# Keys and values of a four-layer attention kernel's third layer: computed in the layer itself, or ahead of it in the second

## The reference

```
q = layer_norm(x) @ q_w + q_b                # 16 heads of 32 columns
k = ctx @ k_w + k_b
v = ctx @ v_w + v_b
h = softmax(q k^T / sqrt(32)) v @ cproj_w + cproj_b + x
x = h + gelu(layer_norm(h) @ fc_w + fc_b) @ proj_w + proj_b
```

## Time and profile before

| | |
|---|---|
| median of three runs | 2687.87 us (2686.5 to 2689.95) |
| the profiled execution | 2687.89 us, span 2686.1 us |
| busy | PE 2477.0 (92%), DVE 1280.0, POOL 1106.1, ACT 1089.2 us |
| grouped layer | about 797 to 1198 us of the span |
| third layer's attention | about 1198 to 1537 us |
| mean granted TensorE clock | 0.967 of full speed |
| DMA | 181.25 MB, mean 67 GB/s |

### The profile page before, as it was taken

The page is one execution under the profiler, slowest core; times in us unless marked ns, Lnnn a source line. Parts: engine busy times, 40 slices in busy tenths (PEclk is TensorE's granted clock), DMA queues, the critical chain, the costliest instruction groups (busy, mean ns, idle before and its releaser), DMA issues.

```text
span 2686.1 us, 47930 instructions
## 1 busy us (share of the span) xinstructions
PE 2477.0 (92%) x18464; PEld 2080.4 (77%) x18464; DVE 1280.0 (48%) x2527; ACT 1089.2 (41%) x3705; POOL 1106.1 (41%) x1972
## 2 busy tenths in 40 slices
PE   7999998999997788758889899999899999899999
PEld 5887886888886666647778788888788888688887
DVE  4555564323226878764555533322355555432322
ACT  4555553111117777754565511111355555311111
POOL 2454446400035888873454571003335444640000
PEclk9999999999998989878999999999999999999999
DMA  4112213111122222221232241102211211311100
GB/s 154 56 56 74 86 48 95 59 47 48 57 71 72 82 91 70 74 67 45 94 111 77 82 129 48 47 23 69 87 48 49 84 53 48 95 59 48 47 32 16
DMA packets 110320, 181.25 MB, mean 67 GB/s; under 512 B 7888, under 2 KB 43408, under 8 KB 109072
## 3 DMA queue, kind: packets, MB, share of 16 engines
q1 hardware_dynamic: 110096, 178.19, 20.2%
HBM read 132.02 MB, written 46.14 MB: 66 GB/s over the span
## 4 chain that ended last, share of the span: by engine, by line
PE 79%; DVE 8%; ACT 6%; POOL 3%; issue 3%; DMA 1%; SPq 0%; DVEq 0%; POOLq 0%; ACTq 0%
PE banks L317 70%; PE banks L453 4%; ACT plain_high L697 4%; PE banks L480 3%; DVE neg_max L948 2%; DVE plain_high L944 2%; POOL plain_high L1268 1%; DVE plain_work L953 1%; PE banks L504 1%; DVE rounded_work L1046 1%; DVE rounded_work L1020 1%; DVE stats L1072 1%; POOL rounded_high L308 0%; PE banks L442 0%; ACT plain_high L684 0%
## 5 line engine op out<-in xcount | busy, mean ns | idle before, releaser
L317 PE MATMUL banks<-rounded_work,rounded_low 128*128 128x512 f32 (+1 forms) x2688 | 534.7, 357 | 58.4 <-issue 35.2
L1268 POOL TENSOR_SCALAR plain_high<-plain_high,inv_sum 128x128 f32<-128x128 f32 (+1 forms) x1024 | 389.6, 403 | 410.2 <-DVE inv_sum L966 409.7
L317 PEld LDWEIGHTS banks<-rounded_work,rounded_low 128*128 128x128 f32 x2688 | 446.7, 200 | 125.6 <-issue 53.7
L317 PE MATMUL banks<-rounded_work,rounded_high 128*128 128x512 f32 (+1 forms) x2400 | 485.4, 356 | 8.4 <-DMA rounded_work<-ctx_split 5.8
L925 ACT ACTIVATE plain_work<-banks,columns 128x512 f32<-128x512 f32 x192 | 132.5, 690 | 865.3 <-PE banks L317 865.3
L317 PEld LDWEIGHTS banks<-rounded_work,rounded_high 128*128 128x128 f32 x2400 | 397.1, 191 | 75.8 <-issue 10.0
L1244 DVE CAST rounded_work<-plain_work 128x512 fp32r<-128x512 f32 x192 | 99.3, 517 | 694.1 <-ACT plain_work L925 682.9
L317 PE MATMUL banks<-rounded_low,rounded_work 128*128 128x512 f32 x1728 | 413.1, 391 | 0.0
L317 PE MATMUL banks<-rounded_high,rounded_work 128*128 128x512 f32 (+1 forms) x1728 | 392.7, 380 | 0.0
L317 PEld LDWEIGHTS banks<-rounded_low,rounded_work 128*128 128x128 f32 x1728 | 322.3, 188 | 68.8 <-issue 3.0
L317 PEld LDWEIGHTS banks<-rounded_high,rounded_work 128*128 128x128 f32 x1728 | 311.8, 190 | 60.4 <-issue 1.4
(11 more groups left out here) (101 smaller groups left out, 3055.3 us busy)
## 6 DMA issues: line engine op xcount, KB each, us to landing
plain_work<-x SPq DMA_DIRECT2D x96, 256.0 KB, 2.8
plain_work<-mlp_w SPq DMA_DIRECT2D x96, 256.0 KB, 2.7
rounded_work<-ctx_split SPq DMA_DIRECT2D x24, 1024.0 KB, 5.9
u<-plain_work SPq DMA_DIRECT2D x48, 256.0 KB, 3.1
plain_work<-u SPq DMA_DIRECT2D x12, 1024.0 KB, 7.2
x<-plain_work SPq DMA_DIRECT2D x48, 256.0 KB, 2.1
plain_work<-attention_w SPq DMA_DIRECT2D x44, 256.0 KB, 2.7
plain_work<-inputs_t SPq DMA_DIRECT2D x8, 1024.0 KB, 8.0
```

The lines of the kernel that those rows point to most:

```text
L317: mm = pe.matmul(dst, lhs(i), rhs(j), start=first and n == 0, stop=last and n == 2, skip_group_check=True)
L1268: last = pool.tensor_scalar(part, part, inv_sum[:, R % 2, r, g:g + 1], 1.0, ALU.mult, ALU.mult)
```

## The change

The third layer's keys and values are computed in the grouped layer, where that layer's context is in `XC` anyway, a pair ahead. For each pair that is two key blocks (24 matmuls of 256 columns each), two value blocks (12 of 512 each), and their evacuation. For pair 0 all four stand at the grouped layer's start; for pair p+1 the key blocks stand behind attend of rounds 0 and 1 of pair p, the values behind attend of round 2 and behind the queries of round 3. The results go to `k_ahead` and `v_ahead`, in two slots that hold the third layer's output weights before, are stored to DRAM (1 MB and 0.5 MB a pair), and are loaded by the third layer into double buffers. In the third layer keys, values and the context load are gone, and the output of row 2p-1 stands ahead of attend of round 0 on TensorE, and on VectorE ahead of the heads. The grouped layer's next context load waits for the last value block. Weight splits move: the third layer's key and value weights to the end of the first MLP, four of its query tiles remain in the grouped layer, four output tiles go to the third layer's start.

The diff, cut (ScalarE's removals in the third layer, which mirror TensorE's, semaphores and index helpers are left out):

```diff
         KT_G = [work(rounded, 16 + 4 * h, 2, 2, 2 * P) for h in range(2)]
-        KT_C = work(rounded, 16, 2, 4, 2 * P)
+        KT_C = [work(rounded, 16 - 8 * h, 2, 4, 2 * P) for h in range(2)]
+        XT_C = work(rounded, 0, 2, FB, 2 * P)
+        k_ahead, v_ahead = slots(rounded, 6, 2, 4, 2 * P), slots(plain, 7, 2, D)
         QT = work(rounded, 48, 2, 4, 2 * P)
...
         y_of = [x_of[1], None, x_of[3], out]
+        keys_of, values_of = (nc.dram_tensor(n, [PAIRS, P, w], F32).ap() for n, w in (("cross_keys", 2048), ("cross_values", 1024)))
         ctx_split = nc.dram_tensor("ctx_split", [PAIRS, P, 2, FB, 2 * P], F32).ap()
...
 
-        for key in (("a", 0), ("m", 0), ("a", 1), ("a", 2), ("m", 2), ("a", 3), ("m", 3)):
-            tile_table[key] = (attention_tiles if key[0] == "a" else mlp_tiles)(L[key[1]])
+        for key, names in ((("a", 0), ("o",)), (("m", 0), None), (("a", 1), ("kv", "q")), (("kv", 2), ("k", "v")), (("o", 1), ("o",)),
+                           (("qo", 2), ("q", "o")), (("m", 2), None), (("a", 3), ("k", "v", "q", "o")), (("m", 3), None)):
+            tile_table[key] = mlp_tiles(L[key[1]]) if names is None else attention_tiles(L[key[1]], names)
             first_tile[key] = count
...
         def pe_queries(pe, y, p, i):
...
                 pe_weights(pe, y, "q")
+            if y.kind == CROSS and i == 0:
+                pe_inputs(pe, y, p)
+            x_t = XT_C if y.kind == CROSS else XC[:, :, :, 2 * P:4 * P]
             key = ("Q", y.n, p, i)
...
                     mm = three_passes(pe, dst[:, j * 256:j * 256 + 256], lambda h: weight(y, "q", h, f, t * P, t * P + P),
-                                      lambda h: XC[:, h, f, 2 * P:4 * P], f == 0, f == FB - 1)
+                                      lambda h: x_t[:, h, f, :], f == 0, f == FB - 1)
             mm.then_inc(filled_by(key), 1)
...
             else:
+                pe.wait_ge(kt_loaded[p % 2], 16 * (p // 2 + 1))
                 for i in range(2):
-                    wait_evac(pe, ("K", y.n, p, i))
                     wait_evac(pe, ("Q", y.n, p, i))
...
             pe_values(pe, y, 0, 0)
+            for i in range(2):
+                pe_keys(pe, L[2], 0, i)
+            for i in range(2):
+                pe_values(pe, L[2], 0, i)
             for p in range(PAIRS):
...
                     pe_keys(pe, y, p + 1, 0)
+                    pe_keys(pe, L[2], p + 1, 0)
                 pe_scores(pe, y, p, 2)
...
                 pe_attend(pe, y, p, 1)
+                if more:
+                    pe_keys(pe, L[2], p + 1, 1)
                 pe_scores(pe, y, p, 3)
...
                 if more:
+                    pe_values(pe, L[2], p + 1, 0)
                     pe_scores(pe, y, p + 1, 0)
...
                     pe_queries(pe, y, p + 1, 1)
+                    pe_values(pe, L[2], p + 1, 1)
             pe_out(pe, y, B - 1)
...
         def pe_cross(pe, y):
...
             for i in range(2):
-                pe_keys(pe, y, 0, i)
-            for i in range(2):
                 pe_queries(pe, y, 0, i)
             pe_scores(pe, y, 0, 0)
-            for i in range(2):
-                pe_values(pe, y, 0, i)
             for p in range(PAIRS):
...
                     pe_turn_x(pe, y, p + 1)
+                if p:
+                    pe_out(pe, y, 2 * p - 1)
                 pe_attend(pe, y, p, 0)
                 if more:
-                    for i in range(2):
-                        pe_keys(pe, y, p + 1, i)
                     for i in range(2):
...
                         pe_turn_u(pe, M[y.n], 0, f)
-                if p:
-                    pe_out(pe, y, 2 * p - 1)
                 if more:
...
                 pe_attend(pe, y, p, 1)
-                if more:
-                    for i in range(2):
-                        pe_values(pe, y, p + 1, i)
             pe_out(pe, y, B - 1)
...
             else:
+                if p and i == 0:
+                    act.wait_ge(k_stored, 16 * p)
                 for j in range(2):
                     t = 2 * i + j
-                    last = act.activation(KT_C[:, 0, t, :], bank(key)[:, j * 256:j * 256 + 256], ACT.Identity, bias=col(y, 4 + t))
+                    last = act.activation(k_ahead[:, 0, t, :], bank(key)[:, j * 256:j * 256 + 256], ACT.Identity, bias=col(y, 4 + t))
                 last.then_inc(hi_done, hi_count(key))
...
                     act_keys(act, y, p + 1, 0)
+                    act_keys(act, L[2], p + 1, 0)
                 act_round(act, y, p, 2, (p, 1), nothing)
...
                 act_heads(act, y, p, 1)
+                if more:
+                    act_keys(act, L[2], p + 1, 1)
                 act_round(act, y, p, 3, (p, 2), nothing)
...
                 act_heads(act, y, p, 2)
+                if more:
+                    act_values(act, L[2], p + 1, 0)
                 act_round(act, y, p + 1, 0 if more else None, (p, 3), nothing)
...
             dve_queries(dve, y, 0, 1)
+            for i in range(2):
+                dve_keys(dve, L[2], 0, i)
             dve.wait_ge(m_stored, 64 * GROUPS)
...
 
+                dve_values(dve, L[2], p, 1)
                 dve_round(dve, y, p, 1, (p, 0), inputs)
...
                     dve_keys(dve, y, p + 1, 0)
+                    dve_keys(dve, L[2], p + 1, 0)
                 dve_round(dve, y, p, 2, (p, 1), nothing)
...
                 dve_heads(dve, y, p, 1)
+                if more:
+                    dve_keys(dve, L[2], p + 1, 1)
                 dve_round(dve, y, p, 3, (p, 2), nothing)
...
                 more = p + 1 < PAIRS
-                dve_values(dve, y, p, 1)
 
                 def inputs():
...
                 dve_round(dve, y, p, 1, (p, 0), inputs)
+                if p:
+                    dve_out(dve, y, 2 * p - 1)
                 dve_heads(dve, y, p, 0)
                 if more:
-                    for i in range(2):
-                        dve_keys(dve, y, p + 1, i)
                     dve_mask(dve, y, p + 1)
...
                         dve_turn_u(dve, M[y.n], 0, f)
-                if p:
-                    dve_out(dve, y, 2 * p - 1)
                 dve_round(dve, y, p + 1, 0 if more else None, (p, 1), nothing)
...
                 pool_bias(pool, y, 2 * p)
-                split_tile(pool, ("a", 2), 2 * p)
+                if p < 4:
+                    split_tile(pool, ("qo", 2), p)
                 pool_norm(pool, y, p, 3)
-                split_tile(pool, ("a", 2), 2 * p + 1)
                 pool_bias(pool, y, 2 * p + 1)
...
         def pool_cross(pool, y):
+            pool.wait_ge(k_stored, 16 * PAIRS)
+            pool.wait_ge(v_stored, 16 * PAIRS)
+            split_tile(pool, ("qo", 2), 4)
+            split_tile(pool, ("qo", 2), 5)
             pool_norm(pool, y, 0, 0)
+            split_tile(pool, ("qo", 2), 6)
+            split_tile(pool, ("qo", 2), 7)
             for p in range(PAIRS):
...
                     split_tile(pool, ("a", 1), i)
+                pool.wait_ge(down_done, base + 8)
+                for i in range(8):
+                    split_tile(pool, ("kv", 2), i)
                 pool.wait_ge(down_done, base + 11)
-                for i in range(8, 12):
-                    split_tile(pool, ("a", 1), i)
+                for i in range(4):
+                    split_tile(pool, ("o", 1), i)
             elif y.n == 2:
...
 
+        def sp_keys_ahead(sp, p):
+            for i in range(2):
+                wait_evac(sp, ("K", 2, p, i))
+            sp.dma_start(keys_of[p], k_ahead.rearrange("p a b c -> p (a b c)").bitcast(F32)).then_inc(k_stored, 16)
+        def sp_values_ahead(sp, p):
+            for i in range(2):
+                wait_evac(sp, ("V", 2, p, i))
+            sp.dma_start(values_of[p], v_ahead.rearrange("p a b -> p (a b)")).then_inc(v_stored, 16)
+        def sp_ahead(sp, p):
+            sp_keys_ahead(sp, p)
+            sp_values_ahead(sp, p)
+        def sp_cross_keys(sp, p):
+            sp.dma_start(KT_C[p % 2].rearrange("p a b c -> p (a b c)").bitcast(F32), keys_of[p]).then_inc(kt_loaded[p % 2], 16)
+        def sp_cross_values(sp, p):
+            sp.dma_start(V_C[p % 2].rearrange("p a b -> p (a b)"), values_of[p]).then_inc(vc_loaded[p % 2], 16)
         def sp_gqa(sp, y):
...
                 sp.dma_start(t, ins[f"L1_xattn_{name}"].rearrange("(a n) -> a n", a=1).broadcast_to([P, D])).then_inc(gb_loaded, 16)
+            sp_ahead(sp, 0)
             for p in range(PAIRS):
...
                 if more:
-                    wait_filled(sp, v_last(y, p))
+                    wait_filled(sp, ("V", 2, p, 1))
                     sp_c(sp, y, p + 1)
...
                     sp_qk_mask(sp, p + 1)
-                load_tile(sp, ("a", 2), 2 * p)
-                load_tile(sp, ("a", 2), 2 * p + 1)
+                if p < 4:
+                    load_tile(sp, ("qo", 2), p)
                 if p:
+                    sp_values_ahead(sp, p)
                     sp_store_h(sp, y, 2 * p - 2)
...
```

(63 more changed lines are left out.)

36 lines of the change are left out of this document (18 added, 18 removed).

## The result

The changed kernel takes 2695.34 us (median of 8 executions, 2692.91 to 2699.35), the kernel before 2687.49 in the same session. The ratio is 1.0029 with an interval of 1.002 to 1.0039: slower by 0.3%, where 2671.0 and faster was forecast. The profiled execution took 2694.84 us, with a span of 2692.8 against 2686.1.

What follows compares the result with a forecast made beforehand. Four engines handing to one another bound the grouped layer, TensorE with almost no cover the third. Grouped layer and start +61.5 us, third layer -78, sum -16.5: 2671 us from 2687.87, range 2644 to 2704.

Steps and rivals of the forecast that it cites:

- the third layer, -78: Third layer: taking out keys and values saves 78 us, bounds -85 to -67.
- the first pair (-7.0): Third layer's first pair: only the keys go, queries start to end falling from 13.8 to 6.8 us, -7.0.
- the six pairs (-62.6): Third layer's six further pairs: each 29.5 us against 39.94, -10.4 a pair, -62.6 in all.
- the last M0 to M1 (-2.7): Third layer's last pair, between its two rows' first maxima on VectorE: -2.7 us without values.
- the piece with two bounds: Third layer's queries: 5.8 us at full clock, 8.0 with a slow first half, 6.8 taken.
- The rival of another wait in this layer: Third layer: in-order chains of ScalarE and VectorE hold the pair near 33 us, 2692 in all; chance 0.12.
- the full-clock sum of the grouped layer: Grouped layer's four rounds with added blocks at full clock: 53.0 us against 46.7, 53.9 on the average pair.
- the charge for the half clock: Grouped layer: half of a block's extra 2.2 us charged, making a pair 55.0 us, +7.4 a pair, +52.
- sign of being wrong: Grouped layer: a pair over 57.5 us would show the forecast wrong.
- the case of slow blocks: Rival, grouped layer: added blocks run slow, 2714 us in all by the author's estimate; chance 0.20.
- Nothing, as said: Grouped and third layers: added stores and loads, 1.5 MB a pair each, costed at nothing.
- The rival that the grouped layer hides more: Grouped layer: idle TensorE time takes added work, a pair of 52 us, 2645 in all; chance 0.13.

Runs made afterwards that it cites:

- e3: Changed kernel with the third layer's moved output projection and its copy put back at their old place in all pairs; 2704.66 us, ratio 1.0061.
- e2: Changed kernel with six useless 512-column matmuls ahead of attend of rounds 1 to 3 in grouped-layer pairs 0 to 6; 2665.91 us, ratio 0.9915.
- e1: Changed kernel with three of the four added grouped-layer blocks issued ahead of attend of rounds 1, 2 and 3, not behind; 2650.33 us, ratio 0.9859.
- e7: e1 with eight useless 512-column matmuls ahead of the first scores of each next pair in the third layer; 2647.65 us, ratio 0.9854.
- e4: Changed kernel with the output projection and its copy back at their old place in the third layer's last pair alone; 2695.41 us, ratio 1.0026.
- e5: e1 with the edit of e4 as well; ratio 0.9866, of three executions of 2649.79 to 2653.61 us.
- e6: Kernel before with the filler of e2, on the grouped layer's query weights; 2690.04 us, ratio 1.0021.

## Why the prediction was wrong

**Right: the third layer, -78.** Its terms came out at -5.8 for the start (forecast -5.9), -4.3 for the first pair (-7.0), -66.0 for the six pairs (-62.6) and -2.1 for the last M0 to M1 (-2.7): -78.2. That the sum agrees to 0.1 is luck: the first pair gave 2.7 less and the six pairs 3.4 more. The queries were the piece with two bounds and came out near the lower one, at 6.0 us, with a wait of 1.28 us ahead of them; in e3 they took 7.43 behind a wait of 3.24, so that both the shorter wait and the shorter queries came with the moved projection. The rival of another wait in this layer fell.

**Right: the full-clock sum of the grouped layer.** 53.9 us a pair was worked out from rows of the kernel before, and e2, which has the change's code at full clock, takes 53.6 to 53.9. The mechanism is right; the closeness is in part luck, since the rounds come to 53.6 where 53.0 was summed, and the 0.9 added for the average pair hardly shows in e2. The start was put at +9.7 and came to +7.3.

**Wrong: the charge for the half clock.** The prediction wrote "I charge half of a block's extra 2.2: 55.0 us". The pair takes 58.0, and e2 puts the clock's part at 29.6 us over seven pairs, 4.2 a pair, where 1.1 was charged. The step failed twice over. The wait came ahead of attend in three rounds of four and every time in pairs 1 to 6 with a slow attend (mostly +0.85) and slow queries or a slow block behind it (+0.6 to +0.8, once +0.95), so it was a term of each of them and no chance event. And the prediction counted on waits of "some 1.7 us ahead of attend"; they are 2.17, 3.07 and 3.05, and in round 0 it had been 0.53 before. The longer rounds made these waits: they let GpSimd get ahead with its normalising, so the turns no longer wait for it, and the work ahead of attend is done sooner while attend still starts at M + 6.8. In round 0 the output projection starts at M + 1.65 (987.25), and started at M + 3.3 in the kernel before (906.57 against 903.28). e1, with its shorter rounds, shows the reverse. The grouped layer of e7 shows both: where round 3 took 13.8 to 14.6 us (three times), the turns behind it don't wait and round 0 takes 13.4; where it took 9.6 us (four times), the turns wait for GpSimd and round 0 takes 15.4 to 17.0. That the length of the round before is the cause is read off these traces; no run changed it alone. The prediction's own sign of being wrong, a grouped pair over 57.5, came up with 58.0. The price of one slow block, on the other hand, was put too high: no run shows the 2.2 us that the charge halves for a block behind attend (nearest is the third layer before, 5.2 us for the first 24 matmuls and 2.88 for later ones). Blocks and queries behind attend's wait took 0.6 to 0.8 us more than at full clock, and in the key block of round 2 only the first part runs at half clock (0.50 for 1.55 us, then 0.98). So the two errors partly cancel.

This was the case of slow blocks, to which the forecast gave a chance of 0.20: in rounds 0, 2 and 3, behind attend's wait, though in round 0 it was the queries and not the added block. At the forecast's 2.2 us, two blocks more a pair, with two attends at 0.86 more (1.94 less 1.08), would be 43 us in seven pairs and 2714 in all, by the author's estimate. The size lies between that and the forecast: 2671 + 21.9 for the clock (29.6 - 7.7) - 2.4 for the start + 4.2 for the end is 2694.7, and the profiled execution took 2694.84.

**The clock in the pair.** In e2 the granted clock rises from 0.91 to 1.00 once TensorE is given something to do in the wait, and falls nowhere in the pair. In the change the blocks were not in the gaps but behind them, and the pair's clock stayed where it was: 0.91, and before 0.89 in the stretch of the earlier trace rows and 0.91 from M(2,0) to M(3,0).

**Nothing, as said.** The stores and loads cost nothing that shows: a DMA share of 0.43 in the third layer's pair, and no wait for them, or for the context, among TensorE's rows of either pair. The rival that the grouped layer hides more (a pair of 52, 2645 us) did not come, for the reason given against it: the idle time lies ahead of attend and the blocks behind it. e1, which moves the blocks there, comes to 51.1 and 2650.

**Wrong and smaller: the end of the third layer** was put at nothing without a reason. It lost 3.8 us. The trace of e4 gives 3.0 of it back with the projection at its old place; the times of e4 and e5 don't confirm any.

## What to carry to other kernels

A bound with two ends that hangs on the granted clock is not to be charged at its middle: look at where the new work lands. Work that goes behind a wait such as these (2.2 to 3.1 us) came out of it at half clock (0.50 to 0.52) here and lies on the path; the same work ahead of the wait fills it, and here that order was worth 45 us, nearly three times the gain that was forecast for the whole change. To see whether a stretch suffers from the clock, fill its wait with useless matmuls: 29 us gained by more work names the cause in one run. Where nothing is gained, as in the kernel before, look first whether the clock rose at all; only then does it clear the clock.

## What the runs showed of the hardware that was not expected

- In the changed grouped layer each of the 18 waits of 2.2 to 3.2 us ahead of attend was followed by work at half clock that cost 1.4 to 1.7 us, and 1.5 us of filler in such a wait, with 1.7 us of it left, was enough to keep the clock at 1.00 in e2, whose rounds were alike to 0.1 us from pair 2 to pair 6. Not every wait of that length is followed so: the kernel before waits 2.42 us ahead of the third layer's last output projection (1537.44), whose 12 matmuls then take 3.02 us at a granted clock of 1.00, while in the kernel after they take 4.48 at 0.64 behind the same wait.
- The same filler was not enough in e6, where the same round took 9.58 us in some pairs, 11.8 in another at a mean of 0.71 and 13.46 in a third at 0.62. And in e7 a stretch in which TensorE was busy for 13.65 of 13.8 us ran at a mean of 0.63, 24 matmuls of 128 columns taking 5.36 us in place of 2.87, with no wait of over 1.33 us ahead of it from 949 us on. The same round ran at 1.00 in the next pair, though the rows ahead are alike: transposes with waits of 1.33 and 0.64 us between them, there 0.99 and 0.64. What makes the difference stays open.
- In the kernel after VectorE's subtraction of 128x512 in the split took 1.64 us three times and its cast 0.83 twice between 1527.7 and 1534.1, while GpSimd had casts and subtractions on tiles of the same size; the medians of the 16 of each are 0.69 and 0.42. No run changed GpSimd's work alone.
